# Every layer norm of an eight-layer network in two halves of 1024 columns instead of four chunks of 512

## The reference, cut to what matters

```python
def _layernorm(x, axis=-1, eps=1e-05):
    m = jnp.mean(x, axis=axis, keepdims=True)
    v = jnp.var(x, axis=axis, keepdims=True)
    return (x - m) / jnp.sqrt(v + eps)

x = _layernorm(x + _L0_attn_ref(x, ...))   # attention with ALiBi
x = _layernorm(x + _L0_ffn_ref(x, ...))    # gated MLP
x = _layernorm(x + _L1_attn_ref(x, ...))   # state space model
x = _layernorm(x + _L1_ffn_ref(x, ...))    # mixture of experts
x = _layernorm(x + _L2_attn_ref(x, ...))   # softmax over queries
x = _layernorm(x + _L2_ffn_ref(x, ...))    # sparse experts
x = _layernorm(x + _L3_attn_ref(x, ...))   # attention with rotary tables
x = _layernorm(x + _L3_ffn_ref(x, ...))    # expert choice
```

## Time and profile before

| | us |
|---|---|
| median of 3 runs (lowest to highest) | 2066.64 (2066.48 to 2067.27) |
| the profiled execution's own time | 2060.97 |
| its span, first to last instruction | 2059.2 |
| PE busy (share of the span) | 1558.2 (76%) |
| DVE busy | 1060.6 (52%) |
| ACT busy | 922.3 (45%) |
| POOL busy | 412.8 (20%) |
| mean granted TensorE clock | 0.873 |

### The profile page before, as it was taken

The page is one execution under the profiler, slowest core; times in us unless marked ns, Lnnn a source line. Parts: engine busy times, 40 slices in busy tenths (PEclk is TensorE's granted clock), DMA queues, the critical chain, the costliest instruction groups (busy, mean ns, idle before and its releaser), DMA issues. The chain is left out here.

```text
span 2059.2 us, 22329 instructions
## 1 busy us (share of the span) xinstructions
PE 1558.2 (76%) x7295; PEld 673.6 (33%) x7295; DVE 1060.6 (52%) x2061; ACT 922.3 (45%) x1541; POOL 412.8 (20%) x369
## 2 busy tenths in 40 slices
PE   4799997998488886676998710291489996699997
PEld 1344443343123332332344300190222222244443
DVE  8577751010079998354775286030388872523332
ACT  4766664321578873211666300020257774233333
POOL 4110110000278884000222002305012110000000
PEclk7899999999589999698999855595679997899999
DMA  5121201000000000001111700106312202000000
GB/s 130 48 56 25 55 10 57 0 0 5 22 2 3 4 5 0 27 0 32 32 32 44 288 8 3 30 20 43 85 57 63 63 18 97 0 5 0 0 0 21
DMA packets 52429, 71.56 MB, mean 35 GB/s; under 512 B 11134, under 2 KB 46102, under 8 KB 50568
## 3 DMA queue, kind: packets, MB, share of 16 engines
q1 hardware_dynamic: 50280, 67.81, 10.8%
q0 software_dynamic: 2048, 2.48, 1.8%
HBM read 48.21 MB, written 18.35 MB: 32 GB/s over the span
## 5 line engine op out<-in xcount | busy, mean ns | idle before, releaser
L656 ACT ACTIVATE a_probs_sb<-a_t_ps 128x512 f32<-128x512 f32 x512 | 286.7, 596 | 127.2 <-PE a_t_ps L537 72.9
L747 DVE CUSTOM_DVE_ANT_0 a_biased<-a_s_ps,a_bias 128x512 f32<-128x512 f32 x256 | 166.2, 686 | 68.0 <-issue 67.9
L533 PE MATMUL a_t_ps<-a_stack 126*128 126x512 bf16 (+1 forms) x512 | 168.3, 391 | 30.9 <-DMA a_stack<-a_least_parts 12.0
L514 PE MATMUL a_s_ps<-a_stack 96*128 96x512 bf16 (+1 forms) x512 | 155.1, 411 | 39.8 <-DMA a_stack<-a_stacks 26.6
L1429 DVE TENSOR_TENSOR_SCAN s_h<-s_dA,s_dbu 128x1024 f32<-128x1024 f32 x64 | 146.6, 2290 | 52.9 <-POOL s_dbu L1394 44.3
L754 DVE TENSOR_REDUCE a_least_sb<-a_s_ps 128x2 f32<-128x1024 f32 x128 | 152.6, 1220 | 33.4 <-PE a_s_ps L514 33.3
L1394 POOL TENSOR_TENSOR s_dbu<-s_du,s_bs 128x1024 f32<-128x1024 f32 x64 | 152.4, 2394 | 29.7 <-DVE s_h L1429 28.0
L2743 ACT ACTIVATE c_hid<-c_up_ps,c_b 128x512 f32<-128x512 f32 x128 | 87.9, 687 | 143.3 <-PE c_up_ps L2712 143.3
L2753 DVE TENSOR_TENSOR c_gated_sb<-c_hid,c_g_ps 128x2048 f32<-128x2048 f32 x32 | 73.2, 2287 | 146.2 <-ACT c_hid L2743 146.2
L552 PE MATMUL a_o_ps<-a_probs_sb,a_vpad 128*16 128x512 f32 x1024 | 137.9, 611 | 0.2 <-ACT a_probs_sb L656 0.2
L2712 PE MATMUL c_up_ps<-xT,c_w 128*128 x256 | 118.0, 604 | 5.7 <-DMA c_select<-in_c_select 5.7
(11 more groups left out here) (428 smaller groups left out, 2566.4 us busy)
## 6 DMA issues: line engine op xcount, KB each, us to landing
x_wu<-in_x_wu SPq DMA_DIRECT2D x2, 4096.0 KB, 16.8
a_stacks<-a_p SPq DMA_DIRECT2D x16, 384.0 KB, 3.0
a_stack<-a_stacks SPq DMA_DIRECT2D x32, 192.0 KB, 3.9
a_stack<-a_stacks SPq DMA_DIRECT2D x64, 96.0 KB, 2.3
a_stacks<-a_p SPq DMA_DIRECT2D x16, 256.0 KB, 2.4
q_q<-q_q SPq DMA_DIRECT2D x32, 128.0 KB, 2.3
x_wd<-in_x_wd SPq DMA_DIRECT2D x2, 2048.0 KB, 33.2
c_w<-in_c_w SPq DMA_DIRECT2D x2, 2048.0 KB, 10.2
```

The costliest lines, as they stand in the source:

```text
L514: made = nc.tensor.matmul(s_ps[:, 2 * (x % 2) + e, :], operand(0, k, pair, e, SCORE_ROWS)[:, t * P:(t + 1) * P], operand(1, k, pair, e, SC ...
L533: last = nc.tensor.matmul(out, operand(1, k, pair, e, TURNED_ROWS)[:, t * P:(t + 1) * P], operand(0, k, pair, e, TURNED_ROWS), start=True, ...
L656: nc.scalar.activation(probs[:, y % PROB_RING, e, :], bank("turned", y, e), ACT.Exp, scale=-1.0).then_inc(probs_ready, 1)
L747: nc.vector.tensor_tensor_reduce(out=biased[:, e, :], in0=s_ps[:, 2 * (x % 2) + e, :], in1=bias[:, h, at:at + N], scale=1.0, scalar=3.0e38 ...
```

## The change

A norm goes through its chain in HALVES = 2 pieces of WIDE = 1024 columns. PE still has to write 512 columns at a time, so each centring or variance step is now two matmuls (four passes), and only the second raises the semaphore. Each Square, Ln, Exp and multiplication covers 1024 columns, over two PSUM banks where it reads PSUM. The semaphore counts follow (`core.norms * HALVES`). The wide-range form is changed in the same way. Nothing else in the program differs; every line of the file behind the norm has moved by 6.

```diff
-    done = core.norms * B
+    HALVES = 2
+    WIDE = T // HALVES
+    done = core.norms * HALVES
...
             def variance(i):
                 pe.wait_ge(square_ready, START + done + i + 1)
-                nc.tensor.matmul(var[:, cols(i)], core.avg[:, :], square[:, cols(i)],
-                                 start=True, stop=True).then_inc(var_ready, 1)
-
-            for i in range(B):
-                nc.tensor.matmul(centred[:, cols(i)], core.centre[:, :], xT[:, cols(i)],
-                                 start=True, stop=True).then_inc(centred_ready, 1)
+                for n in range(WIDE // N):
+                    at = cols(i * (WIDE // N) + n)
+                    last = nc.tensor.matmul(var[:, at], core.avg[:, :], square[:, at], start=True, stop=True)
+                last.then_inc(var_ready, 1)
+
+            for i in range(HALVES):
+                for n in range(WIDE // N):
+                    at = cols(i * (WIDE // N) + n)
+                    last = nc.tensor.matmul(centred[:, at], core.centre[:, :], xT[:, at], start=True, stop=True)
+                last.then_inc(centred_ready, 1)
                 if i > 0:
                     variance(i - 1)
-            variance(B - 1)
+            variance(HALVES - 1)
...
-                nc.scalar.activation(square[:, cols(i)], centred[:, cols(i)], ACT.Square).then_inc(square_ready, 1)
+                nc.scalar.activation(square[:, cols(i, WIDE)], centred[:, cols(i, WIDE)], ACT.Square).then_inc(square_ready, 1)
...
-            for i in range(B):
+            for i in range(HALVES):
                 dve.wait_ge(rstd_ready, START + done + i + 1)
-                nc.vector.tensor_tensor(out[:, cols(i)], centred[:, cols(i)], rstd[:, cols(i)], ALU.mult)
+                nc.vector.tensor_tensor(out[:, cols(i, WIDE)], centred[:, cols(i, WIDE)], rstd[:, cols(i, WIDE)], ALU.mult)
```

More of the change, by code:

```diff
@@ L125, in squares @@
                 act.wait_ge(centred_ready, START + done + i + 1)
-                nc.scalar.activation(square[:, cols(i)], centred[:, cols(i)], ACT.Square).then_inc(square_ready, 1)
+                nc.scalar.activation(square[:, cols(i, WIDE)], centred[:, cols(i, WIDE)], ACT.Square).then_inc(square_ready, 1)
             def log(i):
                 act.wait_ge(var_ready, START + done + i + 1)
-                nc.scalar.activation(logvar[:, cols(i)], var[:, cols(i)], ACT.Ln,
+                nc.scalar.activation(logvar[:, cols(i, WIDE)], var[:, cols(i, WIDE)], ACT.Ln,
                                      bias=core.eps[:, 0:1]).then_inc(logvar_ready, 1)
@@ L134, in root @@
                 act.wait_ge(logvar_ready, START + done + i + 1)
-                nc.scalar.activation(rstd[:, cols(i)], logvar[:, cols(i)], ACT.Exp,
+                nc.scalar.activation(rstd[:, cols(i, WIDE)], logvar[:, cols(i, WIDE)], ACT.Exp,
                                      scale=-0.5).then_inc(rstd_ready, 1)
@@ L143, in _ @@
                         log(i - 1)
-                log(B - 1)
+                log(HALVES - 1)
                 nc.scalar.preload_act_table_set("exp_and_others")
-                for i in range(B):
+                for i in range(HALVES):
                     root(i)
@@ L154, in _ @@
                         root(i - 1)
-                log(B - 1)
-                root(B - 1)
+                log(HALVES - 1)
+                root(HALVES - 1)
         @block.vector
         def _(dve):
-            for i in range(B):
+            for i in range(HALVES):
                 dve.wait_ge(rstd_ready, START + done + i + 1)
-                nc.vector.tensor_tensor(out[:, cols(i)], centred[:, cols(i)], rstd[:, cols(i)], ALU.mult)
+                nc.vector.tensor_tensor(out[:, cols(i, WIDE)], centred[:, cols(i, WIDE)], rstd[:, cols(i, WIDE)], ALU.mult)
 HEADS = 16
```

## The result

| | median (lowest to highest) | runs |
|---|---|---|
| before | 2061.68 us (2057.11 to 2067.27) | 20 |
| changed | 2069.29 us (2065.23 to 2074.77) | 20 |
| ratio, with its 95% interval | 1.0038 (1.0028 to 1.0048) | |

The changed kernel is slower by 0.38%, or 7.8 us (5.8 to 9.9 us). The forecast was slower by 9.5 us and 2076.1 us in a range of 2072.0 to 2080.2. The kernel before is in these 20 runs 5 us faster than in the three whose median the prediction started from, which are its three highest; the other 17 have a median of 2061.02 us.

What follows compares the result with a forecast made beforehand. Each norm was taken to lie on the path as PE fill, ACT work and a last DVE step. Six plain norms +8.3, wide-range norm +0.3 and clock +0.9 made +9.5 us: 2066.64 to 2076.1 us, range 2072.0 to 2080.2.

Steps and rivals of the forecast that it cites:

- the sum: Whole kernel: the norm and clock terms total +9.5 us, added to the three-run median of 2066.64 us.
- the level: Starting point: the median, 5.7 us above the profiled execution's 2060.97 us, was taken as the base for the forecast.
- The fill: Start of each plain norm: first logarithm waits for six more PE passes, 2.58 us later.
- The stretch from the first logarithm: Plain norm, first logarithm to last multiplication's end: 5.65 us after the change, 6.84 before.
- The plain norm's +1.39: Net growth of one plain norm: 2.58 + 5.65 - 6.84 us; six norms +8.3 us.
- s_ln: The wide-range norm: PE at 2.4 GHz from its first pass, growth of +0.3 us.
- The clock behind f_ln: Stage after f_ln: longer PE idleness makes it start at 1.2 GHz; 0 to 1.7 us, middle 0.9 taken.
- full price: Stage after f_ln: four passes at 1.2 GHz instead of 2.4 GHz cost 1.7 us.
- The rises inside the norms: Clock rises within plain norms may come earlier or later: taken as zero, about 2 us either way in the range.
- The fixed costs that are paid half as often: Rival, ACT and DVE in plain norms: fewer instructions save 7.1 us, giving 2059.5 us; chance 3%.
- absorbed: Rival, stages after norms: they wait for something else, so time stays near 2066.6 to 2069 us; chance 6%.
- The clock costs in more places: Rival, behind and inside norms: longer PE idleness and late clock rises give 2080 us; chance 17%.

Runs made afterwards that it cites:

- e10: Changed kernel plus one or two unused PE matmuls after most stages, ahead of the norms, none behind norms: 2062.73 us, ratio to before 1.0014.
- e11: Kernel before plus one or two unused PE matmuls after most stages, ahead of the norms, none behind norms: 2055.42 us, ratio 0.9972.
- e1: Kernel before with only PE's order changed, all four centring matmuls and then the four variances: 2072.79 us, ratio to before 1.0062.
- e4: Changed kernel plus four unused PE matmuls at the end of each norm: 2060.07 us, ratio to before 1.0005.
- e7: Changed kernel plus four unused PE matmuls behind each norm and one or two after most stages: 2053.11 us, ratio to before 0.9978.
- e9: Changed kernel plus two unused PE matmuls behind each norm and one or two after most stages: 2059.35 us, ratio to before 0.9992.
- e0: Kernel before, unchanged, run once more for a second profiled execution: 2059.44 us, one run.
- e3: Kernel before with the last piece of the six plain norms done in two pieces of 256 columns: 2060.15 us, ratio to before 0.9991.
- e6: Kernel before plus two unused PE matmuls behind each norm and one or two after most stages: 2051.79 us, ratio to before 0.9968.

## Why the prediction was right and wrong

**The failing step is in the sum: the level.** The profiled execution took 2060.97 us and the median of three runs was 2066.64. I wrote that nothing in the norms explains the 5.7 us and added 9.5 us to the median. With more runs the kernel before stands at 2061.68 (20 runs) and at 2058.9 to 2059.4 us beside the experiments. The profiled execution was the typical one and the three runs, though within 0.8 us of one another, were all high. The same sum on the profiled execution, 2070.5 us, is 1.2 us from the measured 2069.29. Of the 6.8 us by which the forecast missed, some 5.0 are this starting point (2066.64 against 2061.68) and some 1.9 are the change, 7.6 us between the medians instead of 9.5. The range had room for the costs of the change and none for its starting point. What made those three runs high was not found out: they have no trace.

**The fill: right.** +2.58 us for six passes. Measured at 2.4 GHz +2.35 (e10 and e11), the rest being that with four pieces PE waits 0.2 us for the first square there. In m, x, c and last_ln, where the clock rose in the norm at a like place, it is +2.47 to +2.57. e1 shows the part of PE's order alone as +1.72.

**The stretch from the first logarithm: right in kind, 0.1 us long.** Expected 5.65 us, measured 5.55 or 5.56 in all six. The steps of ACT were taken too long: exponential to logarithm 0.96 us (339.18 to 340.14) instead of 1.04, logarithm to exponential 1.13 (340.14 to 341.27) instead of 1.15. Six times 0.1 us are 0.6 us. The plain norm's +1.39 is +1.19 to +1.29 in the four norms where the clock rose at a like place, +1.05 with the clock kept.

**s_ln: the work right, the clock left out.** Expected +0.3, measured +2.12, because the clock was at 1.2 GHz in most of its first eight passes (stretch 517). Where it stayed high, in e4's trace, s_ln is 13.02 us long, +0.42 on 12.60. The prediction took the clock to stay high there, from one trace. It falls in four of the five traces with the changed norm (14.71 or 14.72 us in the changed kernel, e7, e9 and e10); with the norm as before it is 12.60 us in six of seven and 14.08 us in e0. Whether the change has a part in where it falls stays open.

**The clock behind f_ln: right in kind, and its bounds too.** The next stage began at 1.2 GHz and grew by 1.8 us, for a full price of 1.7, of which the sum took half; e4 took that away by filling the idleness. That the kernel before pays it in some of its executions was argued from a_ln; e0 shows it at 2.56 us of idleness, and e1 and e3, whose idleness is 2.57 and 2.42 us, pay 1.4 and 1.5 us. The length of the idle stretch doesn't decide alone: after 4.32 us in e10 the stage began at 2.4 GHz.

**The rises inside the norms: taken as zero, plus or minus 2 us.** f_ln's first part grew by 1.2 us more than the fill, and between e0 and the first profile of the same kernel it differs by +1.0 (f) to -0.9 us (a). e11, which only keeps the clock up ahead of the norms, is 0.28% or 5.8 us faster than before: so much hangs on it. In the profiled pair the clock in the norms, s_ln's included, went against the change (11.3 us in the norms instead of 8.6). The medians are 7.6 us apart, less than the norms of that pair; which terms are smaller in the other executions no trace shows.

**The rivals.** The fixed costs that are paid half as often are real: 1.29 us a norm come back from ACT and DVE. They don't decide, since the fill costs 2.35 us or more. (The prediction's pair of rows for such a cost, 1008 and 597 ns, reads PSUM; the pair that reads SBUF, 1046 and 617 ns in the earlier trace rows, shows it as well.) Nothing was absorbed: f's stage begins 0.45 us behind the last multiplication in both kernels, and behind the five other norms this distance is the same in both traces within 0.01 us. *The clock costs in more places* came true in part in the profiled pair: the work behind x_ln began at 1.2 GHz instead of 2.4, though that stage as a whole is 2.2 us shorter. The Trainium skill's rule that idle gaps let the clock fall ("TensorE: Matmul & The Clock Gate", section "HAM oscillation — how this bites in real kernels") agrees with the filled kernels, which gained 5 to 7 us by it. The traces don't bear it out gap by gap: the clock fell soon after 1.70 us of idleness in e6, and after 4.32 us in e10 it was still up when the work began.

## What to carry to other kernels

The norm here is as long as its fill on PE, its work on ACT and its last step on DVE; larger pieces shortened only the middle. A short pipeline over several engines can be read in the same three parts. Before merging pieces, count what the first result of the next engine has to wait for, in the order in which the engine ahead of it issues. Before a time is forecast from a few runs, look at how the profiled execution stands to them: if they differ by more than the effect, the range has to take in both levels.

## What the runs showed that I had not expected

- The same program, after the same idle stretch of 2.56 us, began its next stage at 2.4 GHz in one execution and at 1.2 GHz in another (f's stage 170.9 and 172.7 us). The 20 runs of the kernel before spread over 10 us.
- Matmuls whose result nobody uses pay: two behind each of seven norms 5.4 us, both fillings 6.6 to 7.2 us, four behind each norm of the changed kernel 6.8 us.
- 32 passes of only 8 columns take 3.91 us nearly all at 2.4 GHz and 6.93 us at 1.2 GHz. Their weight loads follow the clock too: most last 0.19 us in e7 and 0.33 us in e9.
- Splitting the last piece into 256 columns gained 0.13 us in f_ln, since its two logarithms, 0.47 us each, start 0.37 us apart (0.84 - 0.47) and not 0.26.
- An activation or multiplication over two PSUM banks takes what its columns say: Square 1.02, Ln 1.11, product 1.23 us for 1024 columns.
